# Ten graph hops on one core: gathers and scatters in runs of three batches, next-row splits on VectorE

## The reference, cut to what matters

```python
def step(f, _):                                   # layer 0, ten times
    msg = f[src] * edge_weight[:, None]
    agg = jax.ops.segment_sum(msg, dst, num_segments=n)
    f = (1.0 - ALPHA) * agg + ALPHA * feat_0
    return (f, None)
out, _ = jax.lax.scan(step, feat, None, length=K)
...
agg = jax.ops.segment_sum(msg, dst, num_segments=n) * cj[:, None]   # layer 2
...
agg = jax.ops.segment_sum(msg, dst, num_segments=N) + b             # layer 3
```

## Time and profile before

| | us |
|---|---|
| median of 3 runs (9559.17 to 9568.19) | 9561.17 |
| span of the profiled execution, first to last instruction | 8923.4 |
| median less span (launch and what lies around the span) | 637.8 |
| the profiled execution's own time | not listed |
| ten hops, within the span | 1790 to 5692 |
| the two single-hop sums | 7923 to 8326, 8415 to 8817 |

### The profile page before, as it was taken

One profiled execution on the slowest core, in us unless ns is written; L12 is line 12 of the kernel. 1 busy time (PEld: TensorE's weight loads), 2 busy tenths in 40 slices (PEclk: granted clock), 3 DMA queues, 4 the chain that ended last, 5 costly groups with the idle time before them and its releaser, 6 DMA issues. The chain is left out here.

```text
span 8923.4 us, 552863 instructions
## 1 busy us (share of the span) xinstructions
PE 7680.2 (86%) x228719; PEld 6445.3 (72%) x228719; DVE 6522.8 (73%) x13003; ACT 4080.7 (46%) x9176; POOL 5562.0 (62%) x5896
## 2 busy tenths in 40 slices
PE   4957757789999999999999999589999999959795
PEld 4856657788989898898989889445444444449794
DVE  5778978888888888888888888644444444478787
ACT  1239969934444444444444444244444444424242
POOL 2520000078888888888888877477777777737473
PEclk9999965599999999999999999799999999979797
DMA  5210035589999999999999999633333323249495
GB/s 80 92 40 0 0 110 227 226 299 318 323 320 322 320 321 320 318 323 317 323 320 324 318 315 323 193 77 80 77 79 78 79 77 77 69 151 323 170 323 161
DMA packets 574277, 1832.02 MB, mean 205 GB/s; under 512 B 215358, under 2 KB 276822, under 8 KB 572638
## 3 DMA queue, kind: packets, MB, share of 16 engines
q1 hardware_dynamic: 493774, 1773.87, 59.9%
q0 software_dynamic: 59776, 46.03, 3.2%
q10 hardware_dynamic: 20624, 10.90, 0.6%
HBM read 1667.67 MB, written 157.79 MB: 205 GB/s over the span
## 5 line engine op out<-in xcount | busy, mean ns | idle before, releaser
L1342 POOL TENSOR_TENSOR arena<-arena 128x768 bf16<-128x768 f32 (+2 forms) x1800 | 2735.4, 1520 | 876.3 <-DVE arena L1413 869.5
L1283 ACT CAST arena<-banks 128x384 bf16<-128x384 f32 (+1 forms) x3600 | 1741.9, 489 | 2725.9 <-DVE banks L1409 2723.0
L1443 PE MATMUL banks<-arena 128*128 128x48 bf16 x58800 | 2469.3, 184 | 1.2 <-issue 1.1
L1443 PEld LDWEIGHTS banks<-arena 128*128 128x128 fp8e4 x58800 | 2316.6, 96 | 0.9 <-issue 0.8
L1455 PE MATMUL banks<-arena 32*128 32x144 bf16 x118800 | 2202.9, 223 | 14.9 <-POOL arena L1342 8.5
L1413 DVE TENSOR_TENSOR arena<-banks,arena 128x384 f32<-128x384 f32 (+1 forms) x3600 | 1924.5, 566 | 332.4 <-ACT arena L1283 191.2
L1443 PE MATMUL banks<-xc,arena 128*128 128x48 bf16 x24500 | 2032.6, 184 | 139.9 <-issue 50.6
L1443 PEld LDWEIGHTS banks<-xc,arena 128*128 128x128 fp8e4 x24500 | 1878.0, 95 | 329.0 <-issue 185.6
L1409 DVE TENSOR_TENSOR banks<-banks,wslot 128x384 f32<-128x384 f32 (+1 forms) x3600 | 1877.0, 567 | 273.3 <-PE banks L1443 231.3
L1455 PEld LDWEIGHTS banks<-arena 32*128 32x128 bf16 x118800 | 1867.6, 93 | 91.1 <-POOL arena L1342 9.8
L1712 POOL DMA_INDIRECT f<-node_table,idx x1568 | 1565.5, 998 | 557.5 <-issue 468.4
(11 more groups left out here) (375 smaller groups left out, 10285.7 us busy)
## 6 DMA issues: line engine op xcount, KB each, us to landing
arena<-onehots SPq DMA_DIRECT2D x1200, 768.0 KB, 4.3
arena<-onehots SPq DMA_DIRECT2D x300, 864.0 KB, 4.5
arena<-onehots SPq DMA_DIRECT2D x300, 800.0 KB, 4.3
arena<-in_dst SPq DMA_DIRECT2D x195, 512.0 KB
onehots<-arena SPq DMA_DIRECT2D x100, 768.0 KB, 3.2
arena<-key_rows SPq DMA_DIRECT2D x196, 196.0 KB
f<-node_table,idx POOLq DMA_INDIRECT x1568
onehots<-arena SPq DMA_DIRECT2D x25, 864.0 KB, 3.5
```

The lines of the kernel that those rows point to most:

```text
L1283: nc.scalar.copy(mp_high[:, b % 3, tiles, :], bank).then_inc(top_done, 1)
L1342: nc.gpsimd.tensor_tensor(mp_low[:, b % 3, 0:NTILE[b], :], mp_rest[:, b % 3, 0:NTILE[b], :], mp_mid[:, b % 3, 0:NTILE[b], :], ALU.subtract ...
L1443: m = nc.tensor.matmul(to, hot[:, i * P:(i + 1) * P], x_part, start=c == 0, stop=c == 2)
```

## The change

What it does:

- TensorE's order becomes: gathers of batches 0 to 2 of the next group, scatters of 3 to 5 of this one, gathers of 3 to 5 of the next, scatters of 0 to 2 of the next. One group per loop turn, as before.
- Each batch has a message buffer of its own (six); those of batches 2 and 3 lie in `src_lo` and `src_hi`.
- The banks are handed over by halves: a gather counts each half as done, VectorE multiplies a half when it is there, and a gather waits per half for the bank of the batch two before. The wait for the gather's one-hots moves from TensorE to ScalarE, which waits for them two batches ahead.
- Gather and scatter one-hots are fetched by separate DMAs, twelve a group in place of six, each into a slot of its own that is free when its own use is over.
- ScalarE copies a group's sums after batch 2 of the next group, and GpSimd adds them in three instructions in a row between batches 2 and 3.
- The split of the next hop's rows moves from GpSimd to the end of VectorE's turn, after batch 5.
- At a hop's start VectorE adds the last group's sums itself, right from the banks, and splits and moves its two tiles before batch 3. The other rows of batch 5 are moved after batch 0. SyncE's table store covers all tiles but these two and is issued after the first group's fetches; ScalarE's store and GpSimd's overflow fetch come after batch 2.

The core of the diff (declarations, semaphores and the single-hop ends are left out):

```diff
@@ SyncE
-                    def fetch(g, d, b):
...
+                    def fetch_gather(g, d, b):
+                        if not isinstance(g, int) or g > 0:
+                            sp.wait_ge(g_done, g * (2 * NBATCH) + (2 * b + 2 - 2 * NBATCH))
...
+                    def fetch_scatter(g, d, b):
+                        if not isinstance(g, int) or g > 0:
+                            sp.wait_ge(s_done, g * NBATCH + (b + 1 - NBATCH))
...
+                    def turn(g, d, before):
+                        for b in FIRST:
+                            fetch_gather(g, d, b)
+                        if before is not None:
+                            for b in SECOND:
+                                fetch_scatter(g - 1, before, b)
+                        for b in SECOND:
+                            fetch_gather(g, d, b)
+                        for b in FIRST:
+                            fetch_scatter(g, d, b)
...
+                        turn(h * NGRP, 0, NGRP - 1 if h else None)
+                        if h:
+                            store_early(h)
+                        turn(h * NGRP + 1, 1, 0)
@@ ScalarE
-                            act.wait_ge(s_done, n + 1)
+                                act.wait_ge(s_done, g * NBATCH + (b + 1 - NBATCH))
...
+                                act.wait_ge(g_in[(b + 2) % NBATCH], g * 16 + (16 if b + 2 < NBATCH else 32))
...
-                                if b == 1 and i == 0 and (not isinstance(g, int) or g > 0):
-                                    copy_sums(g)
...
+                            if enters and b == 0:
+                                move(before_last, g - 1)
+                            if b == FIRST[-1]:
+                                if enters:
...
+                                    act.wait_ge(added_up, 3 * g + 3)
...
+                                    act.dma_start(table_v[:, LAST_TILE:NB, :], accD[:, LAST_TILE:NB, :]).then_inc(x_stored, 16)
+                                elif not isinstance(g, int) or g > 0:
+                                    copy_sums(g - 1)
@@ GpSimd
-                    def split_rest(g, d):
...
-                    def split_low(g, d):
...
+                            pool.wait_ge(r_done[b], g * 2 + 4)
+                            nc.gpsimd.tensor_tensor(mp_low[b], mp_rest[b], mp_mid[b], ALU.subtract).then_inc(lo_done[b], 1)
+                            if b == (2 if opens and h else 0):
+                                gather_overflow(g, h if opens else 0)
+                            if not opens and b == FIRST[-1]:
...
                                 for c in range(3):
+                                    add_up(g - 1, d - 1, c)
@@ VectorE
+                    def split_next(g, d, h):
                         cols = bass.ds(d * (QB4 * D), QB4 * D)
+                        if h:
+                            dve.wait_ge(rest_moved, MOVES * h)
+                            dve.sem_inc(move_seen, 1)
                         dve.wait_ge(added_up, g * 3 + 6)
                         nc.vector.tensor_tensor(next_rest[:, cols], accD_raw[:, cols], acc_top[:, cols], ALU.subtract).then_inc(next_resting, 1)
                         dve.wait_ge(next_resting, g + 1)
                         nc.vector.tensor_tensor(next_low[:, cols], next_rest[:, cols], next_top[:, cols], ALU.subtract).then_inc(next_split, 1)
...
+                    def enter(g, h):
+                        dve.wait_ge(added_up, 3 * g)
+                        add_last(g - 1, added_up, 3 * g)
+                        dve.sem_inc(evac, 1)
+                        nc.vector.tensor_tensor(x_rest[:, last_rows], accD_raw[:, last_rows], acc_top[:, last_rows], ALU.subtract).then_inc(rest_moved, 1)
+                        nc.vector.tensor_copy(x_raw[:, last_rows], accD_raw[:, last_rows]).then_inc(x_moved, 1)
+                        dve.wait_ge(rest_moved, MOVES * h)
+                        nc.vector.tensor_tensor(rest_low[:, last_rows], x_rest[:, last_rows], rest_top[:, last_rows], ALU.subtract).then_inc(next_resting, 1)
...
+                            if enters and b == SECOND[0]:
+                                enter(g, h)
...
                             for i in range(2):
+                                dve.wait_ge(g_done, g * (2 * NBATCH) + (2 * b + i + 1))
+                                if NTILE[b] > NSRC[b] and i == 1:
...
+                            if leaves and b != LATE:
+                                move(batch(b), h, EARLY_GROUPS)
+                            if enters and b == 0:
+                                move(before_last, h - 1, NGRP - 1)
+                        if (not isinstance(d, int) or d > 0) and h + 1 < hops:
+                            split_next(g - 1, d - 1, h)
@@ TensorE
                     def gather(g, b):
-                        pe.wait_ge(ring_in[b], g * 16 + 16)
-                        pe.wait_ge(r_done, (g * NBATCH + (b + 1)) * 2)
-                        pe.sem_inc(g_seen, 1)
+                        freed, turns = (b - 2) % NBATCH, 0 if b >= 2 else -1
...
+                            if i % half == 0:
+                                pe.wait_ge(r_done[freed], (g + turns) * 2 + (2 + i // half + 1))
+                                pe.sem_inc(g_seen, 1)
...
                     def scatter(g, b):
+                        pe.wait_ge(s_in[b], g * 16 + 16)
+                        pe.sem_inc(g_seen, 1)
...
                     with pe.Fori(0, groups - 1) as g:
-                        for b in range(NBATCH):
-                            gather(g + (b + 2) // NBATCH, (b + 2) % NBATCH)
+                        for b in FIRST:
+                            gather(g + 1, b)
+                        for b in SECOND:
                             scatter(g, b)
+                        for b in SECOND:
+                            gather(g + 1, b)
+                        for b in FIRST:
+                            scatter(g + 1, b)
+                    for b in SECOND:
                         scatter(groups - 1, b)
```

More of the change, by code:

```diff
@@ L1236, in store @@
-                    def store(h, first, last, groups):
+                        sp.dma_start(g_ring[b].bitcast(F32), gs[bass.ds(d * P, P), BATCH_AT[b]:BATCH_AT[b] + G_COLS[b]]).then_inc(g_in[b], 16)
+                    def fetch_scatter(g, d, b):
+                        if not isinstance(g, int) or g > 0:
+                            sp.wait_ge(s_done, g * NBATCH + (b + 1 - NBATCH))
+                            sp.sem_inc(slot_seen, 1)
+                        sp.dma_start(s_ring[b].bitcast(F32), gs[bass.ds(d * P, P), BATCH_AT[b] + G_COLS[b]:BATCH_AT[b] + BATCH_COLS[b]]).then_inc(s_in[b], 16)
@@ new lines, in turn, with store_early @@
+                    def turn(g, d, before):
[8 more added lines that the diff above has]
+                            fetch_scatter(g, d, b)
+                    def store_early(h):
@@ L1250, in _ @@
+                        turn(h * NGRP + 1, 1, 0)
                         with sp.Fori(2, NGRP) as d:
-                            for b in range(NBATCH):
-                                fetch(d + h * NGRP, d, b)
+                            turn(d + h * NGRP, d, d - 1)
+                    for b in SECOND:
+                        fetch_scatter(hops * NGRP - 1, NGRP - 1, b)
                 @block.scalar
@@ L1293, in _ @@
                             turn(d + h * NGRP, h, False, False)
-                        turn(h * NGRP + NGRP - 1, h, h + 1 < hops, False)
+                        turn(h * NGRP + NGRP - 1, h, h + 1 < hops, False, h + 1 == hops)
                 @block.gpsimd
@@ new lines, in add_last @@
+                    def add_last(g, done, n):
+                        last = slice((NGRP - 1) * QB4 * D, NGRP * QB4 * D)
+                        here, start = (v[:, last].rearrange("p (q f) -> p q f", q=QB4) for v in (accD_raw, frm))
+                        dve.wait_ge(s_done, g * NBATCH + NBATCH)
+                        for c in range(3):
+                            nc.vector.tensor_tensor(here, here if c else start, banks[:, 4:8, SUM_PARTS[c]], ALU.add).then_inc(done, 1)
+                            dve.wait_ge(done, n + c + 1)
@@ L1422, in _ @@
                         turn(h * NGRP + NGRP - 1, NGRP - 1, h, h + 1 < hops, False)
-                    dve.wait_ge(s_done, hops * NGRP * NBATCH + 3)
-                    last = slice((NGRP - 1) * QB4 * D, NGRP * QB4 * D)
-                    here, start = (v[:, last].rearrange("p (q f) -> p q f", q=QB4) for v in (accD_raw, frm))
-                    for c in range(3):
-                        nc.vector.tensor_tensor(here, here if c else start, banks[:, 4:8, SUM_PARTS[c]], ALU.add).then_inc(last_added, 1)
-                        dve.wait_ge(last_added, c + 1)
+                    add_last(hops * NGRP - 1, last_added, 0)
                 @block.tensor
```

195 lines of the change are left out of this document (89 added, 106 removed).

## The result

| | before | after |
|---|---|---|
| median, us | 9564.68 (9559.17 to 9568.21, 4 runs) | 9858.19 (9848.35 to 9870.35, 4 runs) |
| ratio, 95% interval | | 1.0307 [1.0293, 1.0321] |
| span of the profiled execution, us | 8923.4 | 9846.5 |

The kernel is slower by 294 us. The sign is as forecast, the size is not: 9640 was forecast, with a range that ended at 9750.

A forecast was written before the change was run, and what follows sets the result against it. TensorE alone was taken to set the 15.10 us group. Split groups +162, hop boundaries -57 and unsplit groups -25 gave +80 us on 9561, stated as 9640 us, with a range of 9410 to 9750.

The forecast's parts named there:

- VectorE's cycle: Groups with the split: VectorE's batches plus the split's wait for GpSimd's subtraction make 15.82 us, 0.72 more than now.
- Rival 1: VectorE's second split instruction does not wait for GpSimd; all 300 groups take 14.77 us, total 9405; chance 0.20.
- TensorE alone: Groups without the split: TensorE needs 14.20 us after saving 0.92 on switches; bank waits and scatter steps make it 14.77.
- Between scatter and scatter ... I take 0.03: TensorE's step between successive scatter batches, with three instructions of its own, costs 0.03 us; bounds 0 and above 0.3.
- the boundary: Change from one hop to the next, nine times: 4.0 us each instead of 10.3, together -57 us; bounds 2 and 10.
- Rival 2: Scatter-scatter steps on TensorE cost 0.3 us each; split groups take 16.36 us, unsplit 15.85, total 9845; chance 0.08.
- The overflow rows arrive before batch 5: At a hop's start: ScalarE's store lands in 3.1 us, so the overflow rows are there in time for batch 5.
- the 3.7 us wait for one-hots: At a hop's start, behind the table store: 3.72 us of the 10.3, hidden once one-hots are fetched three runs ahead.
- The clock: TensorE's stall of about 1.4 us before the third gather leaves its clock at 2.4 GHz; nothing charged.
- rival 3: TensorE's clock falls after each stall, 1.6 us in each of 216 groups: +346 us, total 9985; chance 0.04.
- Hidden waits: ScalarE's one-hot waits, SyncE's twelve DMAs a group and GpSimd's three additions in a row are moved at no cost.
- the cover of 0.4 us: GpSimd's additions with the copy take 2.7 us; batch 3 leaves VectorE 3.1 us after the last scatter, so they hide.

The follow-up runs named there:

- the plain copy: GpSimd's indirect overflow gather replaced by a plain DMA of the table's first 128 rows: ratio to before 1.0008 in the kernel after, 0.9844 in the kernel before.

## Why the prediction was wrong in size

Step by step, from the second profiles of both kernels, which have the holes. (They are of chips 3 and 8, on which the kernel before takes 9652 and 9657 us.) A split group is one of the 225 in the nine hops that split rows for a next hop:

| term | predicted, us | measured, us |
|---|---|---|
| 225 split groups | 225 x (15.82 - 15.10) = +162 | 225 x (16.77 - 15.62) = +259 |
| 75 others | 75 x (14.77 - 15.10) = -25 | 75 x (15.91 - 15.62) = +22 |
| 9 boundaries | 9 x (4.0 - 10.3) = -57 | 9 x (7.4 - 8.7) = -12 |
| sum | +80 | +269 |

The timed difference on chip 8 is 284 us. Of the remaining 15, 5 lie in the edge MLP; the rest is not assigned.

**VectorE's cycle: right.** Without the disturbance a split group takes 15.73 to 15.75 us, forecast 15.82. The second split instruction waits for GpSimd: it takes 1.46 us and ends 0.22 to 0.24 us behind GpSimd's subtraction, 216 times of 216 in each profile of the kernel after. The Trainium skill, SBUF - State Buffer, section "Who interferes with whom", says that a VectorE instruction with two SBUF inputs and a GpSimd instruction that reads SBUF exclude each other; all 216 times agree. Taking the split away gives 15.91 for 16.77. Rival 1 (it does not wait) is out.

**TensorE alone: right to 0.13.** Groups without the split take 14.90 us with the plain copy, forecast 14.77. Fewer switches are real, but worth 0.20 us a group (15.10 less 14.90), since most of the 0.92 goes to waits for banks: 0.41 and 0.10 us from one matmul's start to the next in the run of gathers over batches 0 to 2, 0.34 in the other.

**What failed: the term for TensorE's run of scatters, "Between scatter and scatter ... I take 0.03", and the row taken for the base, 15.10 us.** The steps themselves cost nothing. But the sum treated a run of scatters as something that only TensorE's own instructions can break, and put what other engines do to it at nothing, without a reason. In its midst stands GpSimd's indirect DMA, which the change left in GpSimd's program and which TensorE's new order moved from the start of a turn of short batches into a run of 196 scatters. There it costs 1.03 us a group. In the old order it costs 0.52, which the first profile did not show. Both together explain the steady groups: -0.08 + 1.03 - 0.52 = 0.43 for the split ones (1.15 - 0.72), 0.13 + 1.01 - 0.52 = 0.62 for the others (0.29 + 0.33). Of the 189 us between +80 and +269 the gather makes 152 (225 x 1.03 + 75 x 1.01 - 300 x 0.52), the boundary 45, and what is left of the groups -8. Rival 2 gave 9845 and lies 13 us from the result, by another mechanism: the size of a loss does not prove its cause.

The gather is not the whole loss. With the plain copy in both kernels, so without holes in either, the ratios are 1.0008 and 0.9844: the change still costs 1.6%, some 158 us. In the ten hops and the two single-hop sums it is 140 us, where the forecast was +80. The groups give 129 of them (225 x 0.64 - 75 x 0.20; forecast 137). A boundary costs 9.7 us (403.1 - 25 x 15.735) against 8.8 (386.3 - 377.5), where 4.0 against 10.3 was forecast: +8 us and not -57. So without the gather the time would have come out near 9720 by these numbers, an estimate, within the stated range, and the boundary would have been the term that failed.

Of the mechanism only this much is shown: it is GpSimd's indirect operation, not its bytes or queue, and TensorE meanwhile waits for nothing that the trace names. The traces show one regularity. The holes open at varying times after the DMA's start, but the last one ends at nearly the same time after it: at a median of 1.30 to 1.34 us in the second profile of the kernel before, both of the kernel after, and the versions with the split on GpSimd and with the later gather, with eight in ten groups between 1.28 and 1.36. So the price depends on how much of these 1.3 us TensorE's order leaves uncovered; why the holes open when they do is open. The Trainium skill's same section says that TensorE and ScalarE never wait on anyone. It speaks of SBUF ports; as a rule for TensorE's pace it fails here, and the measured holes decide. What the two engines share, and why the execution in the first profile was spared, stays open.

**The boundary: too hopeful.** It costs 7.4 us, not 4.0. These are ScalarE's store of the last rows, and the overflow gather and row that wait for it, in the second profile of the kernel after:

```profile
L1328 ACTq DMA_DIRECT2D node_table<-arena x9: 327/349/375, 2242.0 to 5655.5; - x9
...
  POOL ov_rows L1364: 69.9, 9
...
DMA to landing us min/median/max: 5.5/5.9/7.1
```

```profile
L1364 POOL DMA_INDIRECT ov_rows<-node_table,idx_now x300: 984/990/1678, 1805.3 to 9819.8; - x150
...
  DVE banks L1443: 62.7, 9
```

A hop recurs every (5655.5 - 2242.0)/8 = 426.7 us, 25 groups of 16.77 are 419.3, the rest is 7.4. The store lands after 5.9 us, not the 3.1 of the earlier trace rows. So GpSimd waits 7.8 us at each boundary, and VectorE 7.0 for the overflow row of batch 5. "The overflow rows arrive before batch 5" is the clause that failed. It did not hold in the kernel before either; in its second profile ScalarE's store and VectorE's overflow row read:

```profile
L1274 ACTq DMA_DIRECT2D node_table<-arena x9: 326/327/345, 2210.2 to 5403.5; - x9
...
DMA to landing us min/median/max: 3.3/5.5/8.2
```

```profile
L1404 DVE TENSOR_SCALAR banks<-ov_rows,wslot x300: 260/271/274, 1822.9 to 9545.0; 128x48 f32<-128x48 f32 x150
...
  DMA ov_rows<-node_table,idx_now: 52.1, 12
```

The median here is 5.5 us, so the 3.1 of the first profile was itself a low base. What adds the rest was not tested; the larger table store (12.5 us to land in the first profile of the kernel after) runs beside it. And nine of the twelve waits for the overflow row stand at the boundaries, 4.7 us each (4.6 in the first profile). The prediction named only the 3.7 us wait for one-hots, which is gone, as forecast; the other wait came behind it all along and grew to 7.0 us. (In the second profile of the kernel before, a hop recurs every 399.2 us and 25 groups are 390.5: 8.7 us.)

**The clock: right in the groups, not at the boundary.** Windows of the second profile of the kernel after, in a hop, and of the first one around a boundary (the column ahead of the last two is the granted clock):

```profile
2300.00:2500.00 200.00, 176.41 (x8247) 166.43 (x8246) 168.26 (x323) 76.50 (x155) 143.58 (x132) 1.00 0.88 290
```

```profile
3930.50:3937.00 6.50, 4.28 (x168) 4.04 (x157) 6.28 (x12) 2.35 (x5) 3.18 (x4) 0.97 0.96 305
3937.20:3939.00 1.80, 1.80 (x66) 1.79 (x68) 1.72 (x5) 0.75 (x2) 1.17 (x2) 0.50 1.03 440
```

Twelve waits of 1.1 us for a bank in that first window leave the clock at 2.4 GHz, so rival 3 is out. Once in a hop, in its last group, the wait for the bank is 2.04 to 2.12 us (five copies stand on VectorE there). In six of nine such places of the first profile and seven of nine of the second the clock falls at the restart or up to 1.6 us behind it and stays at 1.2 GHz for some 3 us, as in the second and third lines; in the others it stays at 2.4. After the next long wait, of 3.3 to 6.0 us in the first group of the next hop, it is down at 1.2 GHz all eighteen times. The Trainium skill's rule of the prediction (TensorE: Matmul & The Clock Gate, section "A second HAM failure mode: psum-queue depth-cycling"), that short idles between groups of matmuls can make the clock swing, is seen in those last groups and nowhere in the steady ones.

**Hidden waits.** ScalarE's waits for one-hots two batches ahead and SyncE's twelve DMAs cost nothing steady, as said. GpSimd's last addition ends at 2312.77 in the first profile, VectorE's last subtraction of batch 3 at 2312.32: the cover of 0.4 us is not there, batch 3's low parts are late by as much. But GpSimd has caught up at batch 4 (it waits 0.24 us for VectorE there), so nothing comes of it.

## What to carry to other kernels

Compare a profile's span with the timed runs before summing against it: if they differ by much, take another profile before believing its pace. When the order on one engine changes, list what the other engines issue inside each new run, DMAs of GpSimd first: an instruction that nobody moved can fall into a worse place. And a good place for an indirect gather is beside a wait that is there anyway; two small moves (gather there, split back on GpSimd) turned a loss of 3% into a gain of 1.5%.

## What the runs showed of the hardware

GpSimd's indirect DMA of 128 rows (0.99 us) holds up the issue of TensorE's short matmuls: 1.03 us in an unbroken run of scatters (two holes, that open 0.3 and 0.6 us after its start), 0.53 or 0.44 us where scatters and gathers alternate (at 0.8 and 0.9), 0.31 us in a run of gathers (at 1.0), 0.18 us behind a wait of 0.41 us, and nothing seen when it starts within a wait of 1.1 us. The last hole ends some 1.3 us after the start wherever it opens. A plain DMA of the same size from GpSimd (0.55 us) costs nothing. One profiled execution had no such holes in its steady groups: its span is 8923 us where 9659 is usual, but 600 us of that difference lie in the edge MLP, and their cause is not shown.
